# A diffusion-style attention and expert block on one core: three groups of loads and writes moved within SyncE's queue in the projection stage

## The chip, the cores and the metric

The kernel runs on one core of a Trainium2 chip. The metric is the device time of one execution in microseconds; less is better. TensorE (PE) multiplies, VectorE (DVE), ScalarE (ACT) and GpSimd (POOL) work element by element, and SyncE (SP) issues nearly all transfers of the stage that matters here.

## The reference, cut to what matters

```python
mod = (_silu(L0_c) @ L0_wmod).reshape(8, 6, 1, -1)
sa, ca, ga, sb, cb, gb = (mod[:, i] for i in range(6))
ga = (2 * (ga >= 0) - 1) * jnp.maximum(jnp.abs(ga), 0.25)     # gb alike
h = _layernorm(x, axis=-1) * (1 + ca) + sa                    # x: (8, 1024, 512)
q, k, v = (h @ w.T + b for each of the three projections)     # 16 heads of 32
x = x + ga * (softmax(q k / sqrt(32), causal) v @ w_o.T + b_o)
h = _layernorm(x, axis=-1) * (1 + cb) + sb
x = x + gb * (routed experts, 4 of 32 with at most 256 tokens each, + shared expert)
```

All of it is float32. The change lies in the first three lines of the block: modulation, layernorm and the projections to q, k and v.

## The kernel before, in words

The kernel is a row of stages, each a block of five instruction streams, one per engine, ordered by semaphores alone. The first stage, `stage_modulate_qkv`, makes the modulation rows, the layernorm and q, k and v; attention, the shared expert with the routing, and the routed experts follow.

The first stage works in 16 units `u` of 512 tokens, two halves for each of the 8 batches: `u = 2 * b + half`. A function `steps` runs the body for batch 0 in straight code, for batches 1 to 6 in a loop on the chip, and for batch 7 in straight code again. In unit `u`:

- PE multiplies the eight q and k outputs (`n` 0 to 7, L641) and the four v outputs (L645). Each output is 12 matmuls, since each float32 operand is split in a high and a low part and three of the products are taken. From output 7 on it puts the transposes of the next unit (L597) between the v outputs. They use two banks in turn, and transpose `k` waits for `lo_done` of transpose `k - 2`.
- DVE first does the layernorm of the next unit (L466 is its first line), then writes the low part of each q and k output (`out_lo`, L536), then, in turn, the low part of the transposed rows (`hT_lo`, L479) and the v outputs (`out_v`, L544).
- ACT takes the root for the layernorm (L426), writes the high part of each q and k output (`out_hi`, L451) and of the transposed rows (`hT_hi`, L432). `out_hi` and `out_lo` are rings of four tiles: before ACT writes output `n` it waits for `qk_out[n % 4]`, the landing of the two stores of the output four before.
- POOL multiplies and adds the modulation rows `mod` to the next unit's x tile (L384, L386). It waits for `mod_in`, the landing of the rows for that batch.
- SP loads the x tile of the unit after the next (L283), loads the modulation rows of the next batch (L287, even units only, once POOL is done with the old ones: `h_done`), stores q and k (L345, two stores for each output) and v (L352).

The modulation itself is six rows for each batch. PE computes them in three pairs: pair 0 before unit 0, pair 1 within unit 0 behind output 6, pair 2 within unit 1 behind output 4 (`PAIR_AT`). `take_pair` on DVE makes them into `rows` (L486 to L493 for pair 1, which needs the sign and the magnitude) and SP stores them to `mod_dram` (`store_rows`, L296). Pairs 1 and 2 are computed in the bank that the transposes also use, so PE waits for `rows_done` before transpose 1 of the next unit in units 0 and 1.

Before its first unit SP loads the condition, the first x tile, the modulation weights of pair 0, the three projection weights `wraw` (L302), the biases and the second x tile. Behind pair 0 it loads the weights of pair 1, stores the rows of pair 0, and issues six small writes that later stages need: zeros to the pads of `h2_dram` and `out`, the initial slots in `info_dram`, and a zero row for `mod_dram` (L311 to L314). ACT makes the high parts of the projection weights (L421) and DVE the low ones (L500), the first before unit 0's transposes, the other two behind them.

Of the kernel before, what the change touches and what calls it, by code (L numbers as in the profile page):

```python
# [14 lines left out]
P = 128  # L15
NB, S, D = 8, 1024, 512
T = NB * S
# [5 lines left out]
UT = UNIT // P  # L23
# [3 lines left out]
HID, HS, CAP = 256, 1024, 256  # L27
# [8 lines left out]
def raw(ap):  # L36

    return ap.bitcast(FP32)


CREDIT = 16
# [165 lines left out]
def stage_modulate_qkv(nc, x, cT, wmod, wqkvT, bqk, bv, mod_dram, qk_dram, v_dram, h2_dram, info_dram, out, bridge):  # L207


    with ExitStack() as ctx:  # L210
# [29 lines left out]
        zero = s.sb("zero", [P, D], FP32)  # L240
        pad_i = s.sb("pad_i", [P, SP_TILES], I32)
        info = s.sb("info", [P, SP_TILES, 2], FP32)
# [5 lines left out]
        rows_done, rows_out = s.sem("rows", False), s.sem("rows_out", False)  # L248
        padded = s.sem("padded", False)
        w_in, w_hi_done, w_lo_done = s.sems("w_in", 3), s.sem("w_hi_done"), s.sem("w_lo_done")  # L250
        consts, pool_own, dve_own = s.sem("consts"), s.sem("pool_own"), s.sem("dve_own")
        x_in, mod_in = s.sems("x_in", 2), s.sem("mod_in")
        var_done, std_done, norm_done, h_done = s.sem("var"), s.sem("std"), s.sem("norm"), s.sem("h")
# [13 lines left out]
        LAST = NB - 1  # L267

        def steps(eng, body):

            for half in range(HALVES):
                body(0, half, True)
            with eng.Fori(1, LAST) as b:
                for half in range(HALVES):
                    body(b, half, True)
            for half in range(HALVES):
                body(LAST, half, half + 1 < HALVES)

        @block.sync
        def _(sp):  # L280
            def load_x(b, half):
                src = x[bass.ds(b, 1), half * UNIT:(half + 1) * UNIT, :]
                sp.dma_start(x_sb[half][:, :, :], src.rearrange("o (t p) d -> p (o t) d", p=P)).then_inc(x_in[half], 16)  # L283

            def load_mod(b):
                for m, j in enumerate((M_SA, M_CA)):
                    sp.dma_start(mod[:, m, :], mod_dram[bass.ds(b, 1), j, :].broadcast_to([P, D])).then_inc(mod_in, 16)  # L287

            def load_pair(n):
                for i, m in enumerate(PAIRS[n]):  # L290
                    sp.dma_start(w_mod[:, :, i, :], wmod[:, m * D:(m + 1) * D].rearrange("(k p) n -> p k n", p=P)).then_inc(wmod_in[i], 16)

            def store_rows(n):
                sp.wait_ge(rows_done, n + 1)
                for i, m in enumerate(PAIRS[n]):
                    sp.dma_start(mod_dram[0:NB, m, :], rows[n][i * LANE:i * LANE + NB, :]).then_inc(rows_out, 16)  # L296

            sp.dma_start(c_sb[:, :, :], cT.rearrange("(k p) b -> p k b", p=P)).then_inc(c_in, 16)
            load_x(0, 0)
            load_pair(0)  # L300
            for j in range(3):
                sp.dma_start(wraw[j][:, :, :], wqkvT[j].rearrange("(k p) n -> p k n", p=P)).then_inc(w_in[j], 16)  # L302
            sp.dma_start(bqk_sb[:, :], bqk[:, :]).then_inc(consts, 16)
            sp.dma_start(bv_sb[:, :], bv[:, :].broadcast_to([P, D])).then_inc(consts, 16)
            load_x(0, 1)
            sp.wait_ge(pair_done, 1)
            load_pair(1)
            store_rows(0)
            sp.wait_ge(pool_own, CREDIT + 4)
            for r in range(CAP // P):  # L310
                sp.dma_start(h2_dram[T + r * P:T + (r + 1) * P, :], zero[:, :]).then_inc(padded, 16)  # L311
                sp.dma_start(out[T + r * P:T + (r + 1) * P, :], zero[:, :]).then_inc(padded, 16)
            sp.dma_start(info_dram.rearrange("(p n) c -> p n c", p=P), info[:, :, :]).then_inc(padded, 16)
            sp.dma_start(mod_dram[NB:NB + 1, :, :].rearrange("b j d -> (b j) d"), zero[0:6, :]).then_inc(padded, 16)  # L314

            def body(b, half, more):
                u = b * HALVES + half
                if isinstance(b, int) and b == LAST and half == 0:
                    sp.wait_ge(w_lo_done, CREDIT + 3)
                    sp.wait_ge(pair_done, len(PAIRS))  # L320
                    sp.wait_ge(rows_out, 16 * 2 * len(PAIRS))
                    for n in range(RING):
                        sp.wait_ge(qk_out[n], CREDIT + 32 * (NQK // RING) * HALVES)
                    for t in range(UT):
                        sp.wait_ge(v_out[t], CREDIT + 16 * HALVES)
                    bridge.load_heads(sp, 0, 0, bridge.qs[0], bridge.ks[0], bridge.vs[0], qk_dram, v_dram)
                    bridge.load_heads(sp, 1, 1, bridge.qs[1], bridge.ks[1], bridge.vs[1], qk_dram, v_dram, keys=False)
                if not more:
                    sp.wait_ge(tr_done, CREDIT + DK * NB * HALVES)
                    bridge.load_heads(sp, 1, 1, bridge.qs[1], bridge.ks[1], bridge.vs[1], qk_dram, v_dram, rest=False)  # L330
                if more or half == 0:
                    if not isinstance(b, int) or b < LAST:
                        sp.wait_ge(tr_done, CREDIT + DK * (u + 1))
                        load_x(b + 1, half)
                        if half == 0:
                            sp.wait_ge(h_done, CREDIT + UT * (u + 2))
                            if isinstance(b, int) and b == 0:
                                sp.wait_ge(rows_out, 32)
                            load_mod(b + 1)
                for n in range(NQK):  # L340
                    sp.wait_ge(elo_done, CREDIT + NQK * u + n + 1)
                    which, g = (QHI, n) if n < NG else (KHI, n - NG)
                    for part, tile in ((0, out_hi), (1, out_lo)):
                        dst = qk_dram[which + part, bass.ds(b * NG + g, 1), :, half * UNIT:(half + 1) * UNIT]
                        sp.dma_start(dst.rearrange("o p t -> (o p) t"), raw(tile[n % RING][:, :])).then_inc(qk_out[n % RING], 16)  # L345
                for t in range(UT):
                    if not more and t == TURNED_AT - NQK:
                        bridge.load_maxima(sp, 0, 0, bridge.qs[0])
                    sp.wait_ge(ev_done, CREDIT + UT * u + t + 1)
                    tok = half * UNIT + t * P  # L350
                    dst = v_dram[bass.ds(b * NG, NG), tok:tok + P, :]
                    sp.dma_start(dst.rearrange("g t j -> t g j"),  # L352
                                 out_v[t][:, :].rearrange("p (g j) -> p g j", g=NG)).then_inc(v_out[t], 16)
                if isinstance(u, int) and u == 0:
                    sp.wait_ge(pair_done, 2)
                    load_pair(2)
                    store_rows(1)
                if isinstance(u, int) and u == 1:
                    store_rows(2)

            steps(sp, body)
            units = NB * HALVES
            sp.wait_ge(rows_out, 16 * 2 * len(PAIRS))
            sp.wait_ge(padded, 16 * (2 * CAP // P + 2))
            for n in range(RING):
                sp.wait_ge(qk_out[n], CREDIT + 32 * (NQK // RING) * units)
            for t in range(UT):
                sp.wait_ge(v_out[t], CREDIT + 16 * units)
# [1631 lines left out]
```

## Time and profile before

| | |
|---|---|
| median of 3 runs | 3142.4 us (3134.63 to 3147.78) |
| profiled execution | 3153.8 us, of which span 3152.0 us |
| busy share of the span: PE, DVE, POOL, ACT | 93%, 67%, 60%, 43% |
| granted PE clock, mean | 0.968 |
| end of the stage changed | about 620 us into the span |

The span is the time from the first to the last instruction of the profiled execution; the rest of its time lies around it. Views of the trace give instructions with their start in microseconds from the span's start, and for an engine's idle time the event that ended it. The granted clock is the share of TensorE's full speed that the throttle gave; 1.00 is 2.4 GHz and 0.50 is 1.2 GHz.

### The profile page before, as it was taken

The numbers are of one execution on the slowest core, as the hardware profiler recorded it, in microseconds if no ns is written. First come the engines' busy times: TensorE is split into PE (matmuls) and PEld (weight loads), VectorE is DVE, ScalarE is ACT, GpSimd is POOL, SyncE is SP. The second block draws the span as 40 slices with busy tenths as digits, with TensorE's granted clock in tenths as the row PEclk, the third lists the DMA queues.
The fourth block names the chain that finished last, engine by engine and source line by source line (L and its number), as shares of the span: only waits on it lengthen the run. The fifth ranks groups of instructions, "written<-read, shape, count | busy, mean of one in ns | idle before, by whom it ended". The sixth has DMA issues, their size and how long they took to land. (4 is left out here: it accounts for less than half of the span.)

```text
span 3152.0 us, 49674 instructions
## 1 busy us (share of the span) xinstructions
PE 2934.1 (93%) x16384; PEld 2169.5 (69%) x16384; DVE 2113.4 (67%) x5338; ACT 1341.7 (43%) x2435; POOL 1876.1 (60%) x1099
## 2 busy tenths in 40 slices
PE   7999999899999999999999389999999999947997
PEld 5788888666666665666665268888887877736775
DVE  6555555577777777777774457888887778736774
ACT  2222222156666665666666233323323322316774
POOL 1332223178788877887888344576667657545564
PEclk9999999999999999999999689999999999978998
DMA  6555556645645654565452332333233232108996
GB/s 228 205 197 189 177 184 190 187 108 132 139 111 116 137 129 110 116 136 130 110 129 50 111 124 95 95 103 98 86 107 103 77 95 93 57 15 258 229 233 132
DMA packets 281371, 419.46 MB, mean 133 GB/s; under 512 B 48399, under 2 KB 132623, under 8 KB 281166
## 3 DMA queue, kind: packets, MB, share of 16 engines
q1 hardware_dynamic: 258638, 383.17, 42.8%
q0 software_dynamic: 22528, 33.72, 5.6%
q8 instruction: 108, 1.77, 0.2%
q14 instruction: 97, 0.79, 0.1%
HBM read 262.33 MB, written 153.01 MB: 132 GB/s over the span
## 5 line engine op out<-in xcount | busy, mean ns | idle before, releaser
L140 DVE CUSTOM_DVE_ANT_0 att_ps_s<-att_ps_s,att_causal 128x512 f32<-128x512 f32 (+1 forms) x992 | 470.7, 504 | 195.6 <-PE att_ps_s L983 195.2
L911 ACT ACTIVATE att_pt<-att_ps_p 128x512 f32<-128x512 f32 (+1 forms) x1024 | 526.1, 588 | 139.3 <-PE att_ps_p L1031 103.1
L983 PE MATMUL att_ps_s<-att_ks,att_qs 96*128 96x512 f32 x1488 | 514.7, 373 | 7.3 <-PEq L210 3.7
L1028 PE MATMUL att_ps_p<-att_qs,att_ks 98*128 98x512 f32 (+3 forms) x1536 | 506.0, 370 | 7.7 <-ACT att_pt L911 7.1
L861 POOL TENSOR_TENSOR att_gathered<-att_gathered,att_pt 128x2048 f32<-128x2048 f32 (+1 forms) x96 | 405.3, 4222 | 41.8 <-ACT att_pt L911 36.8
L854 POOL TENSOR_TENSOR att_pt<-att_pt 128x1024 f32<-128x1024 f32 (+2 forms) x160 | 345.4, 2159 | 74.8 <-PE att_ps_o L993 49.3
L146 DVE TENSOR_REDUCE att_lower<-att_ps_s 128x1 f32<-128x512 f32 x496 | 340.0, 685 | 71.5 <-PE att_ps_s L983 71.5
L1028 PEld LDWEIGHTS att_ps_p<-att_qs,att_ks 98*128 98x128 f32 x1536 | 272.6, 191 | 154.9 <-issue 106.8
L1306 POOL DMA_INDIRECT slot_info<-ffn_info,ffn_slot x256 | 272.7, 1065 | 123.5 <-issue 78.8
L983 PEld LDWEIGHTS att_ps_s<-att_ks,att_qs 96*128 96x128 f32 x1488 | 276.8, 191 | 81.0 <-DVE att_rowmax L140 23.8
L384 POOL TENSOR_TENSOR qkv_x<-qkv_x,qkv_mod 128x512 f32<-128x512 f32 x60 | 83.5, 1391 | 383.9 <-DVE qkv_x L474 383.9
L993 PE MATMUL att_ps_o<-att_pt,att_vs 128*32 128x512 f32 (+3 forms) x3072 | 288.6, 493 | 0.2 <-ACT att_pt L914 0.2
L1270 POOL TENSOR_TENSOR ffn_h<-ffn_h,ffn_mod 128x512 f32<-128x512 f32 x48 | 75.4, 1570 | 263.5 <-DVE ffn_h L1424 263.5
L1589 PE MATMUL ffn_ps_m<-ffn_dn_hi,ffn_a_hi 128*128 128x512 f32 x512 | 208.2, 407 | 6.1 <-DVE ffn_a_lo L1550 6.1
L858 POOL TENSOR_TENSOR att_gathered<-att_pt 128x2048 f32<-128x2048 f32 x32 | 146.5, 4578 | 100.3 <-ACT att_pt L911 100.3
L1589 PE MATMUL ffn_ps_m<-ffn_hT_hi,ffn_up_hi 128*128 128x512 f32 x512 | 202.3, 395 | 3.5 <-issue 3.5
L536 DVE SCALAR_TENSOR_TENSOR qkv_out_lo<-qkv_ps_m,qkv_bqk,qkv_out_hi 128x512 fp32r<-128x512 f32 x120 | 87.0, 745 | 175.4 <-ACT qkv_out_hi L451 175.4
L451 ACT ACTIVATE qkv_out_hi<-qkv_ps_m,qkv_bqk 128x512 fp32r<-128x512 f32 x128 | 87.9, 688 | 274.0 <-PE qkv_ps_m L641 157.0
L641 PE MATMUL qkv_ps_m<-qkv_hT_hi,qkv_w_hi 128*128 128x512 f32 x512 | 201.3, 393 | 1.4 <-DVE qkv_hT_lo L479 1.4
L1589 PE MATMUL ffn_ps_m<-ffn_hT_lo,ffn_up_hi 128*128 128x512 f32 x512 | 200.5, 392 | 2.2 <-issue 2.0
L1589 PE MATMUL ffn_ps_m<-ffn_dn_hi,ffn_a_lo 128*128 128x512 f32 x512 | 202.5, 395 | 0.0
L1589 PE MATMUL ffn_ps_m<-ffn_hT_hi,ffn_up_lo 128*128 128x512 f32 x512 | 200.6, 392 | 1.5 <-issue 1.5
(290 smaller groups left out, 6836.4 us busy)
## 6 DMA issues: line engine op xcount, KB each, us to landing
att_qs<-qk_parts SPq DMA_DIRECT2D x96, 512.0 KB, 6.9
att_ks<-qk_parts SPq DMA_DIRECT2D x96, 512.0 KB, 12.8
qk_parts<-qkv_out_hi SPq DMA_DIRECT2D x128, 256.0 KB, 2.6
qk_parts<-qkv_out_lo SPq DMA_DIRECT2D x128, 256.0 KB, 2.9
qkv_x<-x SPq DMA_DIRECT2D x16, 1024.0 KB, 5.7
v_rows<-qkv_out_v SPq DMA_DIRECT2D x64, 256.0 KB, 2.3
att_vs<-v_rows SPq DMA_DIRECT2D x32, 512.0 KB, 16.1
o_parts<-att_o SPq DMA_DIRECT2D x64, 256.0 KB, 6.3
```

The source lines that it names most:

```text
L140: dve.tensor_tensor_reduce(part, part, self.causal[:, UNIT - (c1 - c0):UNIT], scale=1.0, scalar=MASKED, op0=ALU.add, op1=ALU.max, accum_ou ...
L146: dve.reduce_max(under[:, low:low + 1], part, axis=AX.X).then_inc(self.max_done, 1)
L641: last = pe.matmul(ps_m[n % BANKS][:, :], w_part[:, k, (n % NG) * P:(n % NG + 1) * P], h_part[:, k, :], start=k == 0 and a + c == 0, stop= ...
L854: pool.tensor_tensor(into, into, tile(c)[:, :, col:UNIT], ALU.add).then_inc(add_done, 1)
L858: pool.tensor_tensor(gathered[:, :, :], tile(4)[:, :, :], tile(5)[:, :, :], ALU.add).then_inc(add_done, 1)
L861: pool.tensor_tensor(into, into, tile(c)[:, :, col:UNIT], ALU.add).then_inc(add_done, 1)
L911: act.activation(tile(c)[:, h, col:UNIT], ps_p[(NPROB * prev.g + n) % NP][:, col:UNIT], ACT.Exp, scale=float(HD) ** -0.5).then_inc(exp_don ...
L983: pe.matmul(bank("s", cur.g, i)[:, 0:c1 - c0], qs[cur.slot][0:STACK, h, t * P:(t + 1) * P], ks[cur.slot][0:STACK, h, c0:c1], start=True, s ...
L993: last = pe.matmul(ps_o[h * HD:(h + 1) * HD, col:UNIT], vs[group.slot][:, kt, h * HD:(h + 1) * HD], tile(c)[:, h, col:UNIT], start=kt == 0 ...
L1028: last = pe.matmul(part[:, i * (UNIT - col):(i + 1) * (UNIT - col)], ks[prev.slot][:, h + i, kt * P:(kt + 1) * P], qs[prev.slot][:, h + i, ...
L1306: pool.indirect_dma_start(info_dram[:, :], bass.IndirectOffsetOnAxis(slot[half][:, j:j + 1].bitcast(U32), 0), info[half][:, j, :], None, b ...
L1589: last = pe.matmul(bank, a[m], c[n], start=i + j == 0, stop=i + 1 == len(pairs) and j == 2)
```

## The change

Three things move in SP's queue; nothing is added or taken away, and no other engine's code changes.

1. The second x tile (`load_x(0, 1)`) is loaded behind the first projection weights instead of behind the biases.
2. The six zero and pad writes become a function `pads`, called behind unit 1's stores and the rows of pair 2, instead of ahead of unit 0.
3. The load of the next batch's modulation rows, with its waits, moves in each even unit from ahead of the q and k stores to between them and the v stores.

```diff
             for j in range(3):
+                if j == 1:
+                    load_x(0, 1)
                 sp.dma_start(wraw[j][:, :, :], wqkvT[j].rearrange("(k p) n -> p k n", p=P)).then_inc(w_in[j], 16)
             sp.dma_start(bqk_sb[:, :], bqk[:, :]).then_inc(consts, 16)
             sp.dma_start(bv_sb[:, :], bv[:, :].broadcast_to([P, D])).then_inc(consts, 16)
-            load_x(0, 1)
             sp.wait_ge(pair_done, 1)
             load_pair(1)
             store_rows(0)
-            sp.wait_ge(pool_own, CREDIT + 4)
-            for r in range(CAP // P):
-                sp.dma_start(h2_dram[T + r * P:T + (r + 1) * P, :], zero[:, :]).then_inc(padded, 16)
-                sp.dma_start(out[T + r * P:T + (r + 1) * P, :], zero[:, :]).then_inc(padded, 16)
-            sp.dma_start(info_dram.rearrange("(p n) c -> p n c", p=P), info[:, :, :]).then_inc(padded, 16)
-            sp.dma_start(mod_dram[NB:NB + 1, :, :].rearrange("b j d -> (b j) d"), zero[0:6, :]).then_inc(padded, 16)
+            def pads():
+                sp.wait_ge(pool_own, CREDIT + 4)
+                for r in range(CAP // P):
...
                     if not isinstance(b, int) or b < LAST:
                         sp.wait_ge(tr_done, CREDIT + DK * (u + 1))
                         load_x(b + 1, half)
-                        if half == 0:
-                            sp.wait_ge(h_done, CREDIT + UT * (u + 2))
-                            if isinstance(b, int) and b == 0:
-                                sp.wait_ge(rows_out, 32)
-                            load_mod(b + 1)
                 for n in range(NQK):
...
+                if half == 0 and (not isinstance(b, int) or b < LAST):
+                    sp.wait_ge(h_done, CREDIT + UT * (u + 2))
+                    if isinstance(b, int) and b == 0:
+                        sp.wait_ge(rows_out, 32)
+                    load_mod(b + 1)
                 for t in range(UT):
...
                 if isinstance(u, int) and u == 1:
                     store_rows(2)
+                    pads()
```

## Rows read from the trace of the kernel before

**Rows 1.** The page, busy time: share of the span and instructions of TensorE.
```profile
PE 2934.1 (93%) x16384; PEld 2169.5 (69%) x16384; DVE 2113.4 (67%) x5338; ACT 1341.7 (43%) x2435; POOL 1876.1 (60%) x1099
```
**Rows 2.** Busy time by stretch: length, each engine, granted clock, DMA share, GB/s.
```profile
185.00:537.00 352.00, 347.22 (x1603) 285.87 (x1603) 189.06 (x361) 79.15 (x130) 106.81 (x80) 1.00 0.54 186
...
625.00:2200.00 1575.00, 1493.89 (x9418) 1005.88 (x9417) 1106.47 (x3283) 824.67 (x1576) 1137.28 (x491) 0.97 0.47 114
```
**Rows 3.** Waits of TensorE, 0 to 620 us: total, times, longest.
```profile
PE qkv_ps_t L597 <- DVE qkv_hT_lo L479: 16.4, 8, 9.7
...
PE qkv_ps_t L597 <- DVE qkv_rows L493: 3.2, 1, 3.2
```
**Rows 4.** SyncE's queue in order of time: start, time in the queue, line.
```profile
2.96 6.04 SPq L302 DMA_DIRECT2D qkv_wraw<-wqkvT  x3
...
32.09 0.36 SPq L311 DMA_DIRECT2D h_rows<-qkv_zero  x1
...
35.42 0.60 SPq L283 DMA_DIRECT2D qkv_x<-x  x1
52.12 0.81 SPq L287 DMA_DIRECT2D qkv_mod<-mod_rows  x2
52.98 0.43 SPq L345 DMA_DIRECT2D qk_parts<-qkv_out_hi  x1
...
116.12 0.43 SPq L283 DMA_DIRECT2D qkv_x<-x  x1
...
173.01 0.33 SPq L345 DMA_DIRECT2D qk_parts<-qkv_out_lo  x1
```
**Rows 5.** DVE in order of time: start, duration, count, idle time before.
```profile
31.34 4.49 DVE L500 TENSOR_TENSOR qkv_w_lo<-qkv_wraw,qkv_w_hi 128x2048 fp32r<-128x2048 f32 x2
...
44.37 2.73 DVE L536 SCALAR_TENSOR_TENSOR qkv_out_lo<-qkv_ps_m,qkv_bqk,qkv_out_hi 128x512 fp32r<-128x512 f32 x4
...
61.37 0.75 DVE L536 SCALAR_TENSOR_TENSOR qkv_out_lo<-qkv_ps_m,qkv_bqk,qkv_out_hi 128x512 fp32r<-128x512 f32 x1 [0.52 <-ACT qkv_out_hi L451]
...
64.38 0.68 DVE L493 SCALAR_TENSOR_TENSOR qkv_rows<-qkv_rows,qkv_mag 64x512 f32<-64x512 f32 x1
```
**Rows 6.** ACT in order of time, idle time before and what ended it.
```profile
29.20 3.70 ACT L421 ACTIVATE qkv_w_hi<-qkv_wraw 128x2048 fp32r<-128x2048 f32 x2
...
44.14 0.69 ACT L451 ACTIVATE qkv_out_hi<-qkv_ps_m,qkv_bqk 128x512 fp32r<-128x512 f32 x1 [2.03 <-PE qkv_ps_m L641]
58.06 0.69 ACT L451 ACTIVATE qkv_out_hi<-qkv_ps_m,qkv_bqk 128x512 fp32r<-128x512 f32 x1 [13.23 <-DMA qk_parts<-qkv_out_lo]
...
162.79 0.69 ACT L451 ACTIVATE qkv_out_hi<-qkv_ps_m,qkv_bqk 128x512 fp32r<-128x512 f32 x1 [2.12 <-PE qkv_ps_m L641]
```
**Rows 7.** TensorE in unit 0: the second pair's matmuls and the transposes behind them.
```profile
52.19 3.63 PE L578 MATMUL qkv_ps_t<-qkv_w_mod,qkv_silu_lane 128*32 128x512 f32 x16
...
65.22 0.63 PE L597 MATMUL qkv_ps_t<-att_ident,qkv_x 128*128 128x128 f32 x4 [3.24 <-DVE qkv_rows L493]
```
**Rows 8.** DMA issues, 0 to 620 us: count, KB each, median us to landing.
```profile
qk_parts<-qkv_out_lo SPq DMA_DIRECT2D x128, 256.0 KB, 2.9
...
qkv_mod<-mod_rows SPq DMA_DIRECT2D x14, 256.0 KB, 3.7
qkv_wraw<-wqkvT SPq DMA_DIRECT2D x3, 1024.0 KB, 13.8
```
**Rows 9.** DVE in order of time: the layernorms run in units 3, 4 and 14.
```profile
149.71 2.46 DVE L466 BATCH_NORM_STATS2 qkv_stats<-qkv_x 128x6 f32<-128x512 f32 x4
184.28 2.46 DVE L466 BATCH_NORM_STATS2 qkv_stats<-qkv_x 128x6 f32<-128x512 f32 x4
...
535.89 2.46 DVE L466 BATCH_NORM_STATS2 qkv_stats<-qkv_x 128x6 f32<-128x512 f32 x4
```
**Rows 10.** POOL in order of time: its first multiply in unit 3.
```profile
154.99 1.52 POOL L384 TENSOR_TENSOR qkv_x<-qkv_x,qkv_mod 128x512 f32<-128x512 f32 x1 [24.72 <-DVE qkv_x L474]
```
**Rows 11.** Busy time by stretch, columns as in rows 2.
```profile
34.00:36.00 2.00, 2.00 (x6) 1.52 (x5) 2.00 (x2) 0.00 (x0) 0.00 (x0) 0.50 0.97 351
...
60.00:70.00 10.00, 6.76 (x34) 5.38 (x33) 7.66 (x13) 3.12 (x6) 0.00 (x0) 1.00 0.73 266
```

More of the change, by code:

```diff
@@ L308, in _ @@
             store_rows(0)
-            sp.wait_ge(pool_own, CREDIT + 4)
-            for r in range(CAP // P):
-                sp.dma_start(h2_dram[T + r * P:T + (r + 1) * P, :], zero[:, :]).then_inc(padded, 16)
-                sp.dma_start(out[T + r * P:T + (r + 1) * P, :], zero[:, :]).then_inc(padded, 16)
-            sp.dma_start(info_dram.rearrange("(p n) c -> p n c", p=P), info[:, :, :]).then_inc(padded, 16)
-            sp.dma_start(mod_dram[NB:NB + 1, :, :].rearrange("b j d -> (b j) d"), zero[0:6, :]).then_inc(padded, 16)
+            def pads():
+                sp.wait_ge(pool_own, CREDIT + 4)
+                for r in range(CAP // P):
+                    sp.dma_start(h2_dram[T + r * P:T + (r + 1) * P, :], zero[:, :]).then_inc(padded, 16)
+                    sp.dma_start(out[T + r * P:T + (r + 1) * P, :], zero[:, :]).then_inc(padded, 16)
+                sp.dma_start(info_dram.rearrange("(p n) c -> p n c", p=P), info[:, :, :]).then_inc(padded, 16)
+                sp.dma_start(mod_dram[NB:NB + 1, :, :].rearrange("b j d -> (b j) d"), zero[0:6, :]).then_inc(padded, 16)
             def body(b, half, more):
```

## The prediction

> **What bounds the kernel now.** The page's first part comes first: TensorE is busy for 93% of a span of 3152.0 us [rows 1]. A microsecond is therefore worth something only where TensorE stands idle or runs at its low clock, and the diff touches only SyncE's queue in the projection stage, the first 620 us or so. The busy time by stretch says how little idle time the loop of that stage holds: 4.78 us of the 352 from 185 to 537 us [rows 2].
>
> TensorE's waits name it [rows 3]. Two kinds belong to the lines changed. One wait, of 3.2 us, is for `rows` from L493, the first of the two modulation pairs computed inside a unit. Eight waits for `hT_lo` sum to 16.4 us. The longest, 9.7 us, is in unit 14, where SyncE is behind the loads of the first attention heads, which the diff leaves alone; one of 1.1 us is in the start-up; the other six, 0.9 to 1.0 us each, lie in units 2, 4, 6, 8, 10 and 12.
>
> Then SyncE's queue shows who is late [rows 4]. In unit 0 its order is: modulation rows for the next batch, then the stores. The modulation rows wait until POOL has read the old ones for unit 1, so they go out at 52.12 and the first store of unit 0 at 52.98, though DVE wrote its first four `out_lo` tiles in a row from 44.37 [rows 5]. The ring of output tiles is four deep, so ACT's fifth output sits 13.23 us behind a store's landing, until 58.06 [rows 6]. DVE works in order: it gets to the seventh output at 61.37 and only then to the pair, whose fifth and last step, L493, starts at 64.38 [rows 5]. TensorE had that pair's matmuls done at 52.19 + 3.63 = 55.8, and stands idle for 3.24 us until 65.22 [rows 7]. The even units of the loop have the same order and repeat this in a weaker form, without a pair.
>
> **Modulation rows behind the stores.** This is the part that pays. With SyncE free, unit 0's first store goes out when `out_lo` 0 is complete, 0.75 us after 44.37, at 45.1 instead of 52.98. Two issues of 0.43 us and a landing of 2.9 us (the median of `out_lo` stores) [rows 4, 8] release ACT's fifth output at 48.9. By the spacing of 2.7 us per output (0.69 of work and 2.03 of waiting) its matmuls are ready at 46.9, so ACT is 2 us late there. For the seventh, ready at TensorE at 52.19, tile 2 must be stored: the third pair of issues ends at 45.1 + 6 x 0.45 = 47.8, landed at 50.7. ACT is back in time. The seventh `out_lo` ends at about 52.2 + 0.7 + 0.8 = 53.7, the pair's matmuls at 55.8, and DVE's five steps for the pair take 3.0 us (from 62.0, where the seventh `out_lo` leaves the engine, to 64.38 + 0.68 = 65.06): `rows` is there at 58.8. TensorE asks for it at 65.22 − 3.24 = 61.98. The idle time is gone with 3 us to spare. Gain: 3.2 us.
>
> For the even units I use the odd ones as the model: they have their stores first and no modulation rows ahead. The layernorms of successive units start at 149.71 and 184.28, and eleven units after the first at 535.89 [rows 9]. An odd unit takes 34.57 us. The eleven are six odd and five even ones, so an even one takes (386.18 − 6 x 34.57) / 5 = 35.75, which is 1.18 more (0.9 to 1.0 as the named wait, the rest in the matmuls that start again behind it). There are six of them in the loop: 7.1 us. In odd unit 3 ACT's fifth output waits 2.12 us, and for TensorE, where the ordinary spacing is 2.03 [rows 6]: with stores on time the ring is just deep enough. Bounds of the term: 0, if the stall only moves, and 7.1, since an even unit has no reason to be quicker than an odd one. It is nearest to the odd unit, so I take 7.1. Unit 14 issues no modulation rows; its 9.7 us stay.
>
> What is late next is the modulation rows themselves. In an odd unit the last store of q and k is issued by 173.01 + 0.33 = 173.3, 23.6 us after its layernorm began [rows 4, 9]. There an even unit will issue its two broadcast loads (0.81 us in the queue), with only v stores behind them. They land 3.7 us later [rows 8], some 28 us into the unit. POOL reads them 5.3 us into the next one (154.99 against 149.71) [rows 10], at 34.6 + 5.3 = 39.9. That leaves 11.8 us of cover. Their other condition, that POOL is through with the old rows, held by 52.12 in unit 0 and will hold before the stores are out, at about 61 (55.8 + 2.7 for output 7, 1.5 for ACT and DVE, 0.9 for its two issues). Cost 0; without cover each further microsecond would cost POOL one in each even unit, and TensorE once POOL's lead over the transposes is eaten.
>
> **Zero writes and pads.** Six issues from 32.09 to 35.4, 3.3 us of SyncE [rows 4]. Nothing behind them is short of time there: the first store is due at 45.1. Taking them away gains 0. In their new place, behind the last store of unit 1 and the last pair's rows, they put off the x tile of unit 4 from 116.12 by 3.3 us, less the 3.2 won in unit 0. That tile is read at 149.71 less the same 3.2, 30 us later. SyncE is free again before the first store of unit 2: in unit 0 the first `out_lo` is complete 9.3 us behind the start of the layernorm (45.1 against 31.34 + 4.49 = 35.8), and the pads begin about when that layernorm does and take 3.3. Their 1.1 MB take some 3 us at the 351 GB/s of the stretch from 34 to 36 us, in which they were written before [rows 11]. Cost 0; without cover 3.3 us, once.
>
> **Second x tile sooner.** It moves from behind all weights and biases to behind the first projection weights. DVE does not wait for it now: its layernorm is next in order behind two weight subtractions that run from 31.34 for 4.49 us [rows 5], and the tile was sent at about 12. No gain. The price is that weights 2 and 3 land one megabyte later, 3.0 us at 351 GB/s. All three issues end by 9.0 and land 13.8 us later (median) [rows 4, 8], so by 23; by 26 they would still be ahead of ACT's use, which is in one row from 29.20 [rows 6]. Cost 0. The modulation weights and the first projection weights keep their place ahead of the tile; were they slowed all the same, the start would pay at most those 3.0 us.
>
> **The clock.** From 60 to 70 us the granted clock is 1.00, the 2.4 GHz level, right through unit 0's idle time; behind the broken-up start it is 0.50, the 1.2 GHz level (34 to 36 us) [rows 11]. So the gap costs its own length and no more, and I add nothing. The Trainium skill (TensorE: Matmul & The Clock Gate, "HAM oscillation") has TensorE fall to half clock behind idle gaps between bursts of matmuls. By that rule unit 0's gap would be followed by a slow stretch like that at the start, some 3 us more to win, and the sum would be 13 us. The trace does not agree at this gap.
>
> **Sum.** 3.2 + 7.1 + 0 + 0 = 10.3 us. The profiled execution, 3153.8 us with 3152.0 of span, would become 3143.5. It lies 11.4 us above the median of the three runs, 3142.4, so I take the sum off the median: 3132 us, 0.33% less. About 0.5%, 15.7 us, is what a measurement of this kernel can tell from no change; the three runs alone spread over 13.2 us.
>
> **Rivals.**
> *Only unit 0 gains.* The even units keep their 1.2 us for a reason of their own, such as v stores put back by the modulation rows. Against it: v tiles are only rewritten a unit later. 3142.4 − 3.2 = 3139. Chance 0.10.
> *Nothing moves.* Stores in unit 0 land so slowly that the pair is late all the same. For that the landing has to grow from 2.9 to over 6 us, while the engines of the DMA are not loaded there. 3142. Chance 0.06.
> *More than the sum.* The attention stage runs at a mean clock of 0.97 [rows 2]; started at another moment it may draw a better or a worse share of the low clock. A hundredth over the 2527 us behind the projections is 25 us; half of it on top of the sum gives 3120. Nothing in the diff steers it. Chance 0.13.
> *Slower: modulation rows too late.* The place is POOL's first multiply behind an even unit. It decides from the point where the rows land 11.8 us later than the 3.7 seen, plus POOL's lead. At 5 us beyond that, seven units pay 35 us, less the 10: 3167. The DMA engines would have to be full, and their share is 0.54 in the loop [rows 2]. Chance 0.04.
> *Start-up pays.* The sooner x tile delays what stands ahead of it: 3132 + 3 = 3135. Chance 0.05.
> The forecast itself keeps 0.62, with a range of its own of 3125 to 3140, for the spread of medians.
>
> **Numbers.** Faster by over 0.5% (below 3126.7): most of the better-clock case and the lower edge of the forecast, 0.17. Slower by over 0.5% (above 3158.1): the late rows or a bad draw, 0.04. Within: 0.79. The range, 3118 to 3146, takes in the forecast, both cases of a smaller gain, the start-up case and a part of the better clock.
>
> **What would show it.** Right: no wait of TensorE for L493; layernorms 34.6 us apart in odd and even units alike; stores of unit 0 from about 45; ACT's fifth output in unit 2 waiting for TensorE instead of a store; modulation rows at about 61, and about 24 us into each even unit; the zero writes at about 112 to 116; unit 14 with its 9.7 us as before; the projections over some 10 us sooner. Wrong: even units at 35.7 still, a wait of POOL for modulation rows, ACT waiting at L421 for weights 2 or 3, or a span that moved by more than the projections did, which would be the clock of later stages.

## The result, and the profile after

| | before | after |
|---|---|---|
| median of 9 runs | 3142.4 us | 3127.5 us (3120.8 to 3135.3) |
| ratio | 1 | 0.9951, interval 0.9936 to 0.9966 |
| profiled execution, its span | 3153.8, 3152.0 us | 3130.5, 3128.6 us |
| last projection matmul starts | 628.2 us | 615.8 us |

The change wins 14.8 us by the medians, 10.7 to 20.1 by the interval. The forecast took 10.3 us off the median, to 3132 us. The measured time is inside the range; the sum is a third too small.

Here and below, a ratio on record is not the quotient of the two medians; the two differ by up to 0.001, which is 3 us. One of the twelve timed runs of e3 took 4090 us at a mean granted clock of 0.648, and its ratio leaves it out.

The code after is three lines longer ahead of the units, so L466 is now L469, L493 is L496 and so on, while the stores' L345 has become L342. TensorE's two largest waits in the projection stage are these (total, times, longest):

```profile
PE qkv_ps_t L600 <- DVE qkv_hT_lo L482: 10.9, 2, 9.8
PE qkv_ps_m L589 <- DMA qkv_w_mod<-wmod: 10.0, 1, 10.0
```

The wait for the pair of unit 0 [rows 3] is gone, and of the eight waits for `hT_lo` two are left: 9.8 us in unit 14 and 1.1 us in the start-up. The 10.0 us are the wait for the first modulation weights, before anything that the change touches. The busy time by stretch says the same: TensorE is idle for nothing in the loop, where it was idle 4.78 us of 352 [rows 2].

```profile
114.00:185.00 71.00, 71.00 (x330) 58.73 (x329) 39.96 (x75) 16.64 (x27) 22.65 (x17) 1.00 0.58 204
185.00:537.00 352.00, 352.00 (x1630) 291.13 (x1629) 195.23 (x366) 81.03 (x132) 112.78 (x86) 1.00 0.57 190
```

SyncE's queue after the change, in order of time, against [rows 4]:

```profile
32.25 0.41 SPq L283 DMA_DIRECT2D qkv_x<-x  x1
45.32 0.36 SPq L342 DMA_DIRECT2D qk_parts<-qkv_out_hi  x1
...
59.94 0.88 SPq L287 DMA_DIRECT2D qkv_mod<-mod_rows  x2
...
110.64 0.35 SPq L313 DMA_DIRECT2D h_rows<-qkv_zero  x1
...
114.79 0.42 SPq L283 DMA_DIRECT2D qkv_x<-x  x1
...
133.24 0.90 SPq L287 DMA_DIRECT2D qkv_mod<-mod_rows  x2
```

Unit 0's first store goes out at 45.32 instead of 52.98, the modulation rows at 59.94, the zero writes from 110.64. In unit 2 the modulation rows go out 24.0 us behind the start of its layernorm. That start is in the next view, DVE's layernorms run in units 0 to 4 and 14, against [rows 9]:

```profile
35.92 2.46 DVE L469 BATCH_NORM_STATS2 qkv_stats<-qkv_x 128x6 f32<-128x512 f32 x4
70.94 2.46 DVE L469 BATCH_NORM_STATS2 qkv_stats<-qkv_x 128x6 f32<-128x512 f32 x4
109.29 2.46 DVE L469 BATCH_NORM_STATS2 qkv_stats<-qkv_x 128x6 f32<-128x512 f32 x4
143.86 2.46 DVE L469 BATCH_NORM_STATS2 qkv_stats<-qkv_x 128x6 f32<-128x512 f32 x4
178.44 2.46 DVE L469 BATCH_NORM_STATS2 qkv_stats<-qkv_x 128x6 f32<-128x512 f32 x4
...
524.17 2.46 DVE L469 BATCH_NORM_STATS2 qkv_stats<-qkv_x 128x6 f32<-128x512 f32 x4
```

From 109.29 to 524.17 twelve units take 414.88 us, 34.57 each, odd and even alike. Before it was 421.89 (114.00 to 535.89): 7.0 us, as reckoned. Unit 0 is the surprise. It takes 70.94 − 35.92 = 35.0 us. Before it took 39.9, by the same two rows of the trace of before:

```profile
35.76 2.47 DVE L466 BATCH_NORM_STATS2 qkv_stats<-qkv_x 128x6 f32<-128x512 f32 x4
...
75.64 2.46 DVE L466 BATCH_NORM_STATS2 qkv_stats<-qkv_x 128x6 f32<-128x512 f32 x4
```

That is 4.9 us, not 3.2. The rest is seen at the start. The matmuls at half clock end at 33.0 us in this profile and at 36.2 in that of before: six of them instead of fourteen, each 0.2 us longer from start to start, so some 1.6 us less. The two profiles also differ behind the projections: the shared expert's stage, from the first to the last of its transposes, takes 939.2 us (1801.5 to 2740.7) before and 927.2 (1790.9 to 2718.1) after. These two surpluses are what the experiments had to explain.

### The profile page after: what moved, and what is told of

It reads as the page before. It is cut to its first block and busy times, and to the rows that moved or that the text cites. A ratio compares the mean times of both kernels' runs of the same rounds, so it can differ in the third digit from the quotient of the medians.

```text
span 3128.6 us, 49674 instructions
## 1 busy us (share of the span) xinstructions
PE 2925.2 (93%) x16384; PEld 2164.9 (69%) x16384; DVE 2117.1 (68%) x5338; ACT 1342.8 (43%) x2435; POOL 1883.1 (60%) x1099
## 5 line engine op out<-in xcount | busy, mean ns | idle before, releaser
L1592 PE MATMUL ffn_ps_m<-ffn_dn_lo,ffn_a_hi 128*128 128x512 f32 x512 | 200.5, 392 | 0.0
L644 PE MATMUL qkv_ps_m<-qkv_hT_hi,qkv_w_lo 128*128 128x512 f32 x512 | 199.9, 390 | 0.0
## 6 DMA issues: line engine op xcount, KB each, us to landing
att_ks<-qk_parts SPq DMA_DIRECT2D x96, 512.0 KB, 12.8
```

The source lines that it names most:

```text
L644: last = pe.matmul(ps_m[n % BANKS][:, :], w_part[:, k, (n % NG) * P:(n % NG + 1) * P], h_part[:, k, :], start=k == 0 and a + c == 0, stop= ...
L1592: last = pe.matmul(bank, a[m], c[n], start=i + j == 0, stop=i + 1 == len(pairs) and j == 2)
```

## The experiments

Two theories had to be told apart first. A: the two stalls are the whole effect, and the surplus is how the low clock happens to fall. B: the moved x tile and pads bring it. A third, C, has a stage behind the projections faster for a reason. e1 to e4 ran on one chip, e5 to e8 on a second, e9 to e12 on a third; each ratio is to the kernel before on the same chip, whose medians were 3141.4, 3114.1 and 3113.1 us.

### e1_mod_only and e10_mod_only_again: the modulation rows alone

```diff
--- before.py
                         load_x(b + 1, half)
-                        if half == 0:
-                            sp.wait_ge(h_done, CREDIT + UT * (u + 2))
-                            if isinstance(b, int) and b == 0:
-                                sp.wait_ge(rows_out, 32)
-                            load_mod(b + 1)
                 for n in range(NQK):
...
+                if half == 0 and (not isinstance(b, int) or b < LAST):
+                    sp.wait_ge(h_done, CREDIT + UT * (u + 2))
+                    if isinstance(b, int) and b == 0:
+                        sp.wait_ge(rows_out, 32)
+                    load_mod(b + 1)
```

> Only the modulation rows move behind the stores; x tile and pads stay as before. Theory A (the two stalls of my sum are the whole effect, the rest is where the low clock happens to fall): unit 0 has no wait for L493, layernorms 34.57 us apart in all loop units, 10 to 12 us faster than before (ratio 0.9962 to 0.9967). Theory B (the moved x tile and pads bring the surplus over the sum): 10 us at most, 4 to 5 us slower than the full change. Theory C (a stage behind the projections is faster for a reason): surplus there only with the full change.

> The modulation rows alone once more, on the same chip as the full change. Theory (x tile and pads are worth nothing): equal to the full change within the intervals, 14 to 16 us faster than before. Rival (they add 4 to 5 us once the stalls are gone): 10 us faster than before, 4 to 5 us slower than the full change.

Measured: 0.9967 (0.9955 to 0.9979), 3130.3 us, and the second time 0.9959 (0.9945 to 0.9972), 3097.3 us. By its medians the first wins 11.1 us, some 4 less than the full change, which left B open. Its trace speaks against B: unit 0 takes 33.7 us, and the last projection matmul starts at 612.8, 15.1 us ahead of the control's on the same chip (627.9, e4 below). Beside the full change on one chip (e11 below, 0.9966, 3100.4 us) the second run is no slower. The modulation rows alone do what the full change does.

### e2_x_pads_only: the x tile and the pads alone

The full change with the load of the modulation rows put back ahead of the stores.

> Only the x tile and the pads move; the modulation rows stay ahead of the stores. Theory A: no difference, within 3 us of before, both stalls as before (3.2 us for L493, 0.9 to 1.0 in each even unit). Theory B: 4 to 5 us faster than before, from the start-up (the low clock behind the first matmuls ends sooner each time).

Measured: 1.0006 (0.9987 to 1.0025), 3141.6 us. Nothing, as A says. But its trace does not show the 3.2 us that both theories took for granted. TensorE's waits from 28 to 530 us:

```profile
PE qkv_ps_t L600 <- DVE qkv_rows L496: 6.0, 1, 6.0
PE qkv_ps_t L600 <- DVE qkv_hT_lo L482: 5.5, 6, 1.0
...
```

### e4_control: the kernel before once more

> The kernel before, once more, as a control: ratio 1.000 with an interval that shows what five rounds can tell. All theories expect the same; its trace shows how far the end of the slow stretch at the start and the length of the shared expert's stage move by themselves. Theory A: by 1 to 3 us and by up to 12 us. Theories B and C: by less than 1 and 3 us.

Measured: 0.9994 (0.9980 to 1.0008), 3140.7 us. Its trace is the key to the surplus. TensorE in unit 0, at the transposes that wait for the pair, and the matmuls behind them:

```profile
64.29 1.09 PE L597 MATMUL qkv_ps_t<-att_ident,qkv_x 128*128 128x128 f32 x4 [6.03 <-DVE qkv_rows L493]
65.03 0.78 PE L645 MATMUL qkv_ps_m<-qkv_w_hi,qkv_hT_hi 128*128 128x512 f32 x1
65.61 0.63 PE L645 MATMUL qkv_ps_m<-qkv_w_lo,qkv_hT_hi 128*128 128x512 f32 x1
...
68.17 0.63 PE L645 MATMUL qkv_ps_m<-qkv_w_lo,qkv_hT_hi 128*128 128x512 f32 x1
...
68.88 0.39 PE L645 MATMUL qkv_ps_m<-qkv_w_hi,qkv_hT_hi 128*128 128x512 f32 x1
```

and busy time by stretch, with the granted clock as the third number from the end:

```profile
32.00:34.00 2.00, 2.00 (x11) 1.65 (x10) 2.00 (x2) 0.04 (x1) 0.00 (x0) 1.00 0.84 319
...
62.00:64.00 2.00, 0.00 (x0) 0.00 (x0) 1.84 (x4) 0.23 (x1) 0.00 (x0) 0.50 0.91 347
...
66.00:68.00 2.00, 2.00 (x6) 1.58 (x5) 0.70 (x2) 0.02 (x1) 0.00 (x0) 0.50 1.02 330
```

Three things differ from the profile that the prediction read. The start is at full clock (1.00 from 32 to 34 us, where [rows 11] has 0.50 for 34 to 36), so TensorE asks for the pair at 58.26, not 61.98. The pair does not come that much sooner: its last step starts at 63.47 instead of 64.38 [rows 5], 0.9 us sooner. It hangs on the stores, and they on the modulation rows, which go out at 51.22 instead of 52.12 [rows 4], 0.9 us sooner as well. So the idle time is 6.03 us, not 3.24. And behind this gap TensorE's clock is at 0.50 (1.2 GHz); the matmuls take 0.63 us until 68.6, where they then take 0.39. Unit 0 takes 41.9 us (layernorms at 34.88 and 76.79). All traces of the experiments start at full clock (the first projection matmul between 28.6 and 30.0 us, no slow one behind it), and in them unit 0 is 41.6 to 41.9 us long with the old order (e2, e4, e5) and 33.6 or 33.7 with the new: 8.3 us by the longer. The shared expert's stage, by its transposes, is 927.1 to 933.3 us in e1 to e4, all on this chip, against 939.2 and 927.2 in the two profiles that came with the change. So this stage moves by 6 us anyway, half of the 12. The 939.2 was seen only once, in an execution that was itself 11.4 us above its kernel's median; why was not found.

### e3_mod_unit0 and e5_mod_loop: each term alone

The modulation rows moved for `b == 0` only, and for the loop only. The diff is against the kernel before and shows the conditions of e3.

```diff
-                        if half == 0:
+                        if half == 0 and not isinstance(b, int):  # e5: isinstance(b, int)
...
+                if half == 0 and isinstance(b, int) and b == 0:       # e5: not isinstance(b, int)
```

> The modulation rows move behind the stores in unit 0 only; the loop keeps them ahead. Theory A: 3.2 us from the wait for L493, up to 5 with a shorter slow stretch at the start; even loop units stay at 35.75. Theory of the clumped stores alone (rival: only unit 0 gains): the same here, and the whole gain of the full change.

> The modulation rows move behind the stores in the loop only; unit 0 keeps them ahead. Theory A: 7.1 us, six even units at 34.57 instead of 35.75, the wait of 3.2 us for L493 as before. Rival (only unit 0 gains): even units at 35.75, nothing gained.

Measured: e3 0.9992 (0.9975 to 1.0010), 3137.8 us; e5 0.9978 (0.9969 to 0.9987), 3106.9 us. e5 wins 7.2 us by its medians and has the 6.0 us wait for the pair and no wait in an even unit: the loop's term, 7.1, is right. e3 is too near to no change for its interval to say more than between 3 us slower and 8 faster. Its trace says it: the layernorms of units 0, 1, 2 and 3 start at 35.27, 68.89, 107.24 and 142.86, so unit 0 is 33.6 us and unit 2 still 35.6, and the projections' last matmul of any kind starts at 620.6, against 627.9 in the control. That is 7.3 us sooner, where e5's, on another chip, is 6.8 sooner (621.1). Neither trace has the 3.2 us that both expectations named: e5 waits 6.0 us for the pair, and e3 gains 8.3 us in unit 0.

### e9_pair_early: the pair freed, the stores left late

```diff
--- before.py
-        PAIR_AT = (6, 4)
+        PAIR_AT = (3, 4)
```

> The kernel before with one number changed: the pair of unit 0 is computed behind output 3 instead of 6, so DVE takes it before it gets stuck behind ACT's fifth output. The modulation rows stay ahead of the stores, which go out as late as before. Theory (unit 0 loses 8.3 us: 6.0 idle for the pair and the rest to the half clock behind it): no wait for L493, no stretch at 0.50 behind it, a wait of 1 to 2 us for hT_lo in its place, unit 0 35 to 36 us long instead of 41.9, even units at 35.75; 6 to 7 us faster than before. Rival (the half clock there has another cause, such as the burst of late stores): the stretch at 0.50 stays, and 4 us at most are won.

Measured: 0.9985 (0.9976 to 0.9994), 3108.6 us, 4.6 us faster by the medians and 1.9 to 7.5 by the interval. The theory had said 6 to 7 and the rival at most 4, so the time does not choose between them; the trace does. TensorE's waits from 55 to 72 us, and its clock there:

```profile
PE qkv_ps_t L597 <- DVE qkv_hT_lo L479: 2.4, 1, 2.4
```

```profile
62.00:64.00 2.00, 0.27 (x2) 0.00 (x0) 1.45 (x3) 1.54 (x3) 0.00 (x0) 1.00 1.04 395
64.00:66.00 2.00, 1.33 (x8) 1.23 (x9) 2.00 (x4) 0.72 (x2) 0.00 (x0) 1.00 1.04 387
```

The stores are as late as before and the DMA engines as full. The wait for the pair is gone, 2.4 us for `hT_lo` stand in its place, and the clock stays at 1.00. Unit 0 is 36.2 us (35.70 to 71.89), 5.7 less than in the control. So it is the long wait, not the burst of stores, that went with the half clock in unit 0. This is one trace against three with the long wait.

### e6_mod_late: the modulation rows past their cover

```diff
--- after.py
-                if half == 0 and (not isinstance(b, int) or b < LAST):
-                    sp.wait_ge(h_done, CREDIT + UT * (u + 2))
...
-                    load_mod(b + 1)
...
                         sp.dma_start(dst.rearrange("o p t -> (o p) t"), raw(tile[n % RING][:, :])).then_inc(qk_out[n % RING], 16)
+                    if n == 0 and half == 1 and (not isinstance(b, int) or b < LAST):
+                        sp.wait_ge(h_done, CREDIT + UT * (u + 1))
...
+                        load_mod(b + 1)
```

> The full change, with the modulation rows later still: in the odd unit, behind the first output's two stores. They land about 9.3 + 1.8 + 3.7 = 14.8 us into that unit, where POOL wants them at 5.3: 9.5 us late, past the 11.8 us of cover. Theory A: POOL waits 9 to 10 us in each of seven units, has some 5 us of lead over the transposes, and TensorE pays 4 to 5 us seven times: 28 to 35 us slower than the full change, 18 to 25 slower than before. Rival (POOL's work has more slack than that): less than 10 us slower than the full change.

Measured: 1.0045 (1.0029 to 1.0061), 3129.1 us, 30.8 us slower than the full change beside it and 14.9 slower than before. TensorE's and POOL's waits from 60 us on:

```profile
PE qkv_ps_t L600 <- POOL qkv_x L389: 18.9, 7, 3.2
```

```profile
POOL qkv_x L387 <- DMA qkv_mod<-mod_rows: 223.6, 7, 32.2
```

Against the full change the size is as expected; against before it is not, since the full change had won more than was reckoned. Of POOL's 32 us per unit it stands idle some 24 in the full change as well. In unit 3 its first multiply starts 13.7 us behind the layernorm instead of 5.3 [rows 9, 10], 8.4 us late, and 3.1 of these reach TensorE.

The make-up is not as expected. TensorE waits 18.9 us in seven places, one of 0.5 us and six of 2.9 to 3.2, instead of 4 to 5 each. The rest comes behind the waits: behind five of the six, 7 to 12 matmuls take 0.63 us instead of 0.39. These are 48 matmuls, each 0.2 us longer from start to start, so some 10 of the other 12 us. Behind the sixth they take 0.39 us at once. Here are two waits of the same length in that one trace, and busy time by stretch behind them:

```profile
239.94 0.65 PE L600 MATMUL qkv_ps_t<-att_ident,qkv_x 128*128 128x128 f32 x4 [2.89 <-POOL qkv_x L389]
...
386.24 1.11 PE L600 MATMUL qkv_ps_t<-att_ident,qkv_x 128*128 128x128 f32 x4 [2.89 <-POOL qkv_x L389]
```

```profile
240.00:243.00 3.00, 3.00 (x16) 2.54 (x17) 0.69 (x1) 0.60 (x1) 0.00 (x0) 1.00 0.32 120
...
386.00:389.00 3.00, 2.76 (x9) 2.38 (x10) 0.69 (x1) 0.60 (x1) 0.11 (x1) 0.50 0.43 159
```

### e8_after_again and e11_after_third: the full change again

> The full change once more, beside the others on the same chip: 10 to 20 us faster than before. Theory A: its slow stretch at the start and its shared expert's stage differ from those of the first profile by as much as those of two profiles of the kernel before. Theory C: the shared expert's stage is again 12 us shorter than before.

> The full change beside the modulation rows alone: 15 us faster than before (8.3 from unit 0, 7.1 from the loop), if unit 0 starts at full clock.

Measured: 0.9952 (0.9940 to 0.9965), 3098.2 us, and 0.9966 (0.9952 to 0.9979), 3100.4 us. Both start at full clock and have unit 0 at 33.7 us. The projections' last matmul starts at 613.1 and 612.9, 14.8 and 15.0 us ahead of the control's 627.9. The shared expert's transposes take 917.8 us in e8, but so they do in e5 on that chip (917.9) and e9 on the third (918.0), which keep a part or all of the old order. In all eight traces of these two chips it is 917.6 to 918.2 us: nothing of the change reaches that stage, and theory C falls.

### e7_heads_behind and e12_heads_mid: the same remedy in unit 14

The largest wait left, 9.7 us, comes from the same place in the queue: the loads of the attention heads ahead of the stores. e7 puts the first heads behind the q and k stores, e12 behind the stores of output 3; both put the second heads behind the v stores. The diff is that of e12; in e7 the first call stands behind the loop over the outputs.

```diff
--- after.py
-                    bridge.load_heads(sp, 0, 0, bridge.qs[0], bridge.ks[0], bridge.vs[0], qk_dram, v_dram)
-                    bridge.load_heads(sp, 1, 1, bridge.qs[1], bridge.ks[1], bridge.vs[1], qk_dram, v_dram, keys=False)
...
                         sp.dma_start(dst.rearrange("o p t -> (o p) t"), raw(tile[n % RING][:, :])).then_inc(qk_out[n % RING], 16)
+                    if n == RING - 1 and isinstance(b, int) and b == LAST and half == 0:
+                        bridge.load_heads(sp, 0, 0, bridge.qs[0], bridge.ks[0], bridge.vs[0], qk_dram, v_dram)
...
+                if isinstance(b, int) and b == LAST and half == 0:
+                    bridge.load_heads(sp, 1, 1, bridge.qs[1], bridge.ks[1], bridge.vs[1], qk_dram, v_dram, keys=False)
```

> The full change, and in unit 14 the first attention heads load behind the q and k stores, the second group behind the v stores, instead of both ahead. Theory (the queue order is the cause of the 9.7 us wait there too): the wait goes, up to 9.7 us faster than the full change, less what the first scores of unit 15 wait for the later heads. Rival (the transfers, 5.6 MB, are the bound and the wait only moves into unit 15): same as the full change.

> The full change, and in unit 14 the first heads load behind the stores of output 3 and the second heads behind the v stores. Theory (loads sent at about 11 us into the unit, when the transfers are light, land before the first scores of unit 15, and q, k and v stores go out in time): neither the 9.7 us wait for hT_lo nor the 7.5 us wait for the heads that took its place in the earlier attempt, 8 to 13 us faster than the full change. Rival (the volume of 5.6 MB is the bound): a wait of 5 us or more comes back elsewhere in units 14 and 15, within 3 us of the full change.

Measured: e7 0.9956 (0.9943 to 0.9969), 3099.1 us, no better than the full change beside it. e12 0.9936 (0.9923 to 0.9950), 3091.6 us, 8.8 us faster than the full change beside it and 21.5 faster than before. Its last projection matmul starts at 606.1, 6.8 us ahead of the full change's. TensorE's longest wait in units 14 and 15, for e7 and then for e12 (from 28 us on):

```profile
PE qkv_ps_t L615 <- DMA att_ks<-qk_parts: 7.5, 1, 7.5
```

```profile
PE qkv_ps_t L614 <- DVE att_rowmax L140: 3.6, 3, 3.3
```

In e7 the stall only moved: the first scores wait 7.5 us for keys sent at 547. In e12 the keys go out at 537.21, when the DMA engines are half busy, and land in time. What is left is a new wait of 3.3 us for DVE at 583.81, with matmuls of 0.63 us behind it until 587.

## Why the prediction was right, and where it was too small

The range, 3118 to 3146 us, also held 3142, no change at all. So it is the traces, more than the time, that bear out the mechanism.

**The loop's term: right.** Reckoned 7.1 us by taking the odd units as the model; e5 measures 7.2, the layernorms 34.57 us apart in all twelve units.

**Unit 0's term: the mechanism right, the size not.** Reckoned 3.2 us. The profiles that start at full clock, all but the two that came with the change, show 8.3: 6.0 of idle time and some 2 us at half clock behind it. The step that mis-sized it is "TensorE asks for it at 61.98": that moment is from one execution with a slow start (0.50 from 30 to 36 us). The pair's moment hangs on POOL and SyncE and hardly on TensorE's clock. In the control TensorE asks 3.7 us sooner and the pair is there only 0.9 sooner, so the gap grows by the other 2.8. With 8.3 in place of 3.2 the sum is 15.4 us. Measured by medians were 14.8, 15.9 and 12.8 for the full change (the last two e8 and e11) and 11.1 and 15.9 for the modulation rows alone (e1 and e10). So 15.4 lies at the upper end. The traces of these four that start at full clock have their last projection matmul 13.4 to 15.1 us ahead of the control's; the two profiles with the slow start are 12.4 us apart there. How many of the timed runs started slow is not on record. That slow starts explain the smaller gains is not shown.

**The clock: wrong for most profiled executions.** "The gap costs its own length and no more" was right for the gap of 3.24 us in the profile of before. It is wrong for the 6.0 us of the three other traces with the old order in unit 0 (e2, e4, e5), all of which have matmuls of 0.63 us behind it. The rule of the Trainium skill (TensorE: Matmul & The Clock Gate, "HAM oscillation"), whose sum was 13 us, came nearer to the measured time. The prediction gave it no chance of its own among its rivals. The trace of before had a second gap that could have been asked, the one of 9.7 us in unit 14, and there it agreed with the rule:

```profile
550.00:560.00 10.00, 10.00 (x47) 8.23 (x47) 0.00 (x0) 0.00 (x0) 7.69 (x10) 1.00 1.07 228
560.00:570.00 10.00, 3.41 (x17) 2.50 (x15) 1.50 (x2) 1.79 (x3) 0.00 (x0) 0.93 1.03 321
570.00:580.00 10.00, 6.92 (x23) 5.67 (x24) 5.27 (x8) 2.88 (x6) 0.33 (x1) 0.55 0.70 244
```

The reader is to see the granted clock at 0.55 behind the idle time, with TensorE back at work.

**Zero writes and pads, and the second x tile: 0, as reckoned.** e2 measures 1.0006, and its interval, 4 us faster to 8 slower, is too wide to exclude the 3.0 us of the start-up rival. Its trace does: the first projection matmul starts at 28.6 us and the last at 626.9, against 29.2 and 627.9 in the control. On top of the rest they add nothing either: the last one starts at 612.8 and 614.5 with the modulation rows alone (e1, e10) and at 613.1 and 612.9 with the full change (e8, e11). ACT still takes weights 2 and 3 in one row from 29.37 without waiting, and DVE's layernorm starts at 35.92, straight behind the weight subtractions. One small claim failed: in unit 2 ACT's fifth output was to wait for TensorE, and waits 2.53 us for a store, half a microsecond more than the usual 2.03:

```profile
122.78 0.69 ACT L454 ACTIVATE qkv_out_hi<-qkv_ps_m,qkv_bqk 128x512 fp32r<-128x512 f32 x1 [2.53 <-DMA qk_parts<-qkv_out_lo]
```

It is so in every trace of the full change (2.50 and 2.64 us in e11 and e8). In e1 and e10, where the pads are early, it waits 2.12 us for TensorE, and in unit 4 of the full change 2.12 as well. The late pads put off the x tile of unit 4 as well: it goes out 3.9 us ahead of unit 2's first store, where e1 has 7.2. Whether the pads or this tile's transfer delays the stores, no run separates. It costs TensorE nothing.

**The cover of the modulation rows: there, and no more than reckoned.** They went out 24.0 us into unit 2, against 23.6, and no engine waited for them; e6 takes the cover away and pays 30.8 us.

**The rivals.** "Only unit 0 gains" fell with e5, "nothing moves" and "start-up pays" with e10 and the trace of e2. "More than the sum" came true in part of its size, but not by its mechanism: the surplus is in unit 0. The shared expert's stage, 12 us shorter in the pair of profiles, does not follow the change in any other trace.

## What to carry to other kernels

In a queue that serves several engines in order, put what has a deadline a whole unit away behind what frees a ring. How far behind is set by when it must land: 24 us into the unit was free here, 19 us later (at 150.32 in e6, 43 us behind unit 2's layernorm) cost 31 us; loads put behind all the stores only moved a stall, put into a quiet stretch ahead of half of them they won 8.8 us. And when an idle time is the distance between two chains, one of them set by TensorE's clock and the other not, read it at both levels of the clock before pricing it from a single profile: here 3.2 us of one execution stood for 8.3 us of the three others that were profiled.

## What the runs showed of the hardware

The length of an idle time alone did not tell whether TensorE's clock fell behind it. It stayed at 1.00 behind gaps of 2.4 us (e9) and 3.24 us (before), and fell behind gaps of 3.1 us (e6: 0.70 from 165 to 170 us), 6.03 us (control: 0.50) and 9.7 us (before, unit 14: 0.55). Within the one execution of e6 it stayed at 1.00 behind a gap of 2.89 us and fell to 0.50 behind another of 2.89 us. So a gap of about 3 us cost its own length alone or, by the count of matmuls at 0.63 us in e6, an estimated 1.4 to 2.4 us more. Every gap of 6 us or more in units 0 and 14 had matmuls of 0.63 us behind it. The same kernel started its first projection matmuls at 0.50 in one profile and at 1.00 in another (before and e4).

The first chip differs from the other two by 0.9% for the kernel before (3141.4 against 3114.1 and 3113.1 us), and a part of it is the shared expert's stage, 931 us on the first (e4) and 918 on the third (e9), another part the 408 and 393 us from its last transpose to the end of the span; why was not examined.
